# Softmax sums in four strips of 32 columns, and a new place for their reciprocal and the norm

## What is computed

```python
q = jnp.einsum('bnd,hde->bhne', query, Wq) * scale
k = jnp.einsum('bmd,hde->bhme', query, Wk)
v = jnp.einsum('bmd,hde->bhme', query, Wv)
logits = jnp.einsum('bhne,bhme->bhnm', q, k)
attn = jax.nn.softmax(logits, axis=-1)
out = jnp.einsum('bhnm,bhme->bnhe', attn, v)
```

## Time and profile before

| | |
|---|---|
| median of 3 runs | 1893.6 us (1893.3 to 1894.4) |
| the profiled execution | 1892.8 us, its span 1891.0 us |
| TensorE busy (matmul) | 97% |
| GpSimd busy | 71% |
| VectorE busy | 64% |
| ScalarE busy | 45% |

### The profile page before, as it was taken

One profiled execution on the slowest core, in us unless ns is written; L12 is line 12 of the kernel. 1 busy time (PEld: TensorE's weight loads), 2 busy tenths in 40 slices (PEclk: granted clock), 3 DMA queues, 4 the chain that ended last, 5 costly groups with the idle time before them and its releaser, 6 DMA issues.

```text
span 1891.0 us, 30738 instructions
## 1 busy us (share of the span) xinstructions
PE 1837.1 (97%) x11400; PEld 1172.4 (62%) x11400; DVE 1212.2 (64%) x2147; ACT 858.9 (45%) x1101; POOL 1346.7 (71%) x719
## 2 busy tenths in 40 slices
PE   7899999999999999999999999999999999999998
PEld 5555555556666565556666565556665555598887
DVE  5566665566766656856666657766666668665565
ACT  3344444444445444443345544444444534465674
POOL 1688787878667867788578767887668677662564
PEclk9899999999999999999999999999999999999999
DMA  4210000002312000022311000021111011533340
GB/s 139 84 41 20 23 18 23 18 23 68 107 29 60 26 18 24 21 63 85 86 44 42 18 13 23 29 81 55 46 44 38 16 34 35 173 110 132 129 134 34
DMA packets 132142, 104.24 MB, mean 55 GB/s; under 512 B 58140, under 2 KB 118684, under 8 KB 130972
## 3 DMA queue, kind: packets, MB, share of 16 engines
q1 hardware_dynamic: 128924, 93.81, 16.7%
q0 software_dynamic: 3072, 8.46, 1.2%
HBM read 69.15 MB, written 29.43 MB: 52 GB/s over the span
## 4 chain that ended last, share of the span: by engine, by line
PE 84%; POOL 5%; DVE 4%; issue 3%; ACT 2%; DMA 1%; SPq 0%; POOLq 0%; DVEq 0%; ACTq 0%
PE score_ps L1134 23%; PE av_ps L1148 22%; PE spare_ps L1097 9%; PE spare_ps L1113 8%; PE spare_ps L1090 5%; PE spare_ps L441 4%; POOL prob_sum L1018 3%; PE y_ps L1713 3%; PE spare_ps L1159 3%; PE h_ps L1684 3%; DVE max_of L1290 1%; PE spare_ps L490 1%; PE spare_ps L465 1%; POOL w_lo L1446 0%; POOL expert_rows L430 0%
## 5 line engine op out<-in xcount | busy, mean ns | idle before, releaser
L1018 POOL TENSOR_TENSOR prob_sum<-prob_sum,probs 128x1024 f32<-128x1024 f32 (+1 forms) x384 | 907.9, 2364 | 193.6 <-ACT probs L1234 161.3
L1290 DVE TENSOR_REDUCE max_of<-spare_ps 128x1 f32<-128x512 f32 x1024 | 656.5, 682 | 346.0 <-PE spare_ps L1113 335.2
L1234 ACT ACTIVATE probs<-score_ps 128x1024 f32<-128x1024 f32 x512 | 502.7, 1025 | 677.1 <-PE score_ps L1134 669.0
L1148 PE MATMUL av_ps<-probs,v 128*64 128x512 f32 x2048 | 487.9, 602 | 2.1 <-ACT probs L1234 1.4
L1148 PEld LDWEIGHTS av_ps<-probs,v 128*64 128x64 f32 x2048 | 129.8, 136 | 240.5 <-issue 218.4
L1014 POOL TENSOR_TENSOR prob_sum<-probs 128x1024 f32<-128x1024 f32 (+1 forms) x64 | 150.4, 2351 | 137.6 <-ACT probs L1234 137.5
L1113 PE MATMUL spare_ps<-k_hi,q_hi 64*128 64x512 f32 x1024 | 229.2, 441 | 14.7 <-DVE max_of L1290 14.0
L1113 PEld LDWEIGHTS spare_ps<-k_hi,q_hi 64*128 64x128 f32 x1024 | 99.1, 185 | 216.1 <-issue 180.4
L1134 PE MATMUL score_ps<-q_hi,k_hi 64*128 64x512 f32 x1024 | 210.9, 406 | 1.1 <-DVE o_in L1340 0.9
L1134 PE MATMUL score_ps<-shift_rows,ones 64*128 64x512 f32 x1024 | 205.3, 394 | 0.0
L1134 PE MATMUL score_ps<-q_lo,k_hi 64*128 64x512 f32 x1024 | 204.7, 393 | 0.0
(11 more groups left out here) (249 smaller groups left out, 2357.7 us busy)
## 6 DMA issues: line engine op xcount, KB each, us to landing
o_transposed<-o_out SPq DMA_DIRECT2D x64, 256.0 KB, 2.0
v<-in_L_ffn_W_dram SPq DMA_DIRECT2D x16, 1024.0 KB, 5.7
o_in<-o_transposed SPq DMA_DIRECT2D x28, 512.0 KB, 4.1
w_raw<-in_L_attn_Wq_dram SPq DMA_DIRECT2D x64, 64.0 KB, 2.3
w_raw<-in_L_attn_Wk_dram SPq DMA_DIRECT2D x64, 64.0 KB, 2.2
wv_raw<-in_L_attn_Wv_dram SPq DMA_DIRECT2D x32, 128.0 KB, 3.2
shift_rows<-neg_rows SPq DMA_DIRECT2D x256, 1.0 KB
x<-in_x_dram SPq DMA_DIRECT2D x4, 1024.0 KB, 5.9
```

Source lines behind the costliest of these rows:

```text
L1018: pool.tensor_tensor(out, out, probs[:, n % RING, heads], ALU.add).then_inc(prob_added, 1)
L1148: last = pe.matmul(av_ps[hd * E:(hd + 1) * E, :], v[:, quad % 2, kt, 2 * first_head + hd, :], probs[:, n % RING, hd, :], start=(kt == 0), ...
L1234: act.activation(probs[:, n % RING], score_ps[n % 2][:, :, :], ACT.Exp).then_inc(probs_ready, 1)
L1290: dve.tensor_reduce(max_of[:, u % 2, kh, j, hd:hd + 1], bank[:, :], AX.X, ALU.max).then_inc(pass_read, 1)
```

## The change

A sum becomes four matmuls instead of two: each head's 512 queries are cut in two `halves` of 256, and each of the four (head, half) gets a strip of 32 of the bank's partitions, with ones of 32 columns. So the result lies in 256 columns instead of 512, and the transpose out of the bank is half as long. The inverse, however, is wanted on all 64 partitions of a head for all 512 queries: eight copies, written as reductions over an axis of one element, bring each strip's 8 columns to both strips of its head (each 32 partitions x 8 elements). A new semaphore counts them, then one reciprocal of 128x16 follows in place, and the spreading as before. In three lines of `STEPS` the words `recip` and `norm` move.

```diff
 STEPS = tuple(tuple(line.split()) for line in (
-    "early av av av pass score score pass sum av recip pass score score pass late bite bite",
-    "bite norm score pass early av pass score score pass score pass late av av av",
-    "av pass score score pass early av sum pass score score pass bite late av recip av",
+    "early av av av pass score score pass sum av pass score score pass recip late bite norm bite",
+    "bite score pass early av pass score score pass score pass late av av av",
+    "av pass score score pass early av sum pass score score pass recip bite late av av",
     "pass norm score score pass early bite bite av pass score score pass late av av av"))
...
+    HALF = BANK // 2
+    HEAD_HALVES = ((0, 0), (0, 1), (1, 0), (1, 1))
...
+    def strip(hd, half):
+
+        return slice((2 * hd + half) * BLOCK, (2 * hd + half + 1) * BLOCK)
...
-                for hd in range(2):
-                    last = pe.matmul(bank[hd * E:(hd + 1) * E, :], ones[:, 0:E], prob_sum[:, u % 2, hd, :],
-                                     start=True, stop=True)
+                for hd, half in HEAD_HALVES:
+                    last = pe.matmul(bank[strip(hd, half), 0:HALF], ones[:, 0:BLOCK],
+                                     prob_sum[:, u % 2, hd, half * HALF:(half + 1) * HALF], start=True, stop=True)
                 last.then_inc(sum_ready, 1)
...
-                dve.transpose(sums[:, :], bank[:, :]).then_inc(sum_turned, 1)
+                dve.transpose(sums[:, 0:HALF], bank[:, 0:HALF]).then_inc(sum_turned, 1)
 
             def invert(u):
                 dve.wait_ge(sum_turned, u + 1)
-                dve.reciprocal(inverse[:, :], sums[:, 0:BANK:BLOCK]).then_inc(recip_done, 1)
+                blocks = HALF // BLOCK
+                for hd, half in HEAD_HALVES:
+                    for other in range(2):
+                        dve.tensor_reduce(inverse[strip(hd, other), half * blocks:(half + 1) * blocks],
+                                          sums[strip(hd, half), 0:HALF:BLOCK].rearrange("p (c a) -> p c a", a=1),
+                                          AX.X, ALU.add).then_inc(sum_copied, 1)
+                dve.wait_ge(sum_copied, 2 * len(HEAD_HALVES) * (u + 1))
+                dve.reciprocal(inverse[:, :], inverse[:, :]).then_inc(recip_done, 1)
                 dve.wait_ge(recip_done, u + 1)
                 dve.transpose(sums[:, :].rearrange("p (c t) -> p c t", t=BLOCK),
```

More of the change, by code:

```diff
@@ L861, in build_attention @@
         sum_turned = sem("sum_turned")
+        sum_copied = sem("sum_copied")
         recip_done = sem("recip_done")
```

## The result

The changed kernel takes 1925.1 us (median of 4 runs, 1924.0 to 1929.9), the kernel before beside it 1894.0 (1893.3 to 1895.1). The ratio is 1.0166, with a 95% interval of 1.0153 to 1.0178. So it is 1.7% slower, where 0.4% faster was forecast, and it lies outside the range. The profiled execution has a span of 1924.4 us against 1891.0: 33.4 more.

What follows compares the result with a forecast made beforehand. TensorE was taken as the bound, busy 1837.1 of 1891.0 us, with VectorE's order mattering inside a half. −19.2 + 11.4 + 0.2 = −7.6 us gave 1885.2 profiled, 1886.0 median, 0.4% faster; range 1874 to 1908.

Steps and rivals of the forecast that it cites:

- The order of TensorE does not change: In the changed `STEPS`, TensorE, ScalarE and GpSimd keep their steps and only VectorE's order moves; no time of its own.
- Term 1, the sum: Sums on TensorE: four strips abreast save 0.427 us, a change of width costs 0.13; 0.30 each, 19.2 us for 64.
- no price for the change of width: Rival at TensorE's sums: changing column width is free, or k1's bank is no bound; 8 to 11 us less, 1876, chance 0.14.
- two at a time: Rival at TensorE's sums: only two strips run abreast, so a sum still streams 0.855 us; 1913 us, chance 0.12.
- abreast with a loss: Rival at TensorE's sums: four strips need 0.55 us rather than 0.43, 8 us in all; 1894, no change, chance 0.09.
- Term 2, the copies: VectorE's work behind a sum: transpose 0.27 us shorter, eight copies 0.09 us apart added; chain through the spreading 1.75 us.
- Term 3, the first line: VectorE's chain behind the first line's last pass delays low parts that free banks: 0.28 us per light half, 11.4 in all.
- VectorE's queue becomes the bound of the pass: Rival in the first line: copies 0.21 us apart, chain 0.85 longer, 24 halves lose 0.85 each; 1906 us, chance 0.15.
- its point of 0.14 us: Distance between VectorE's copies from which the slower rival decides, at 0.32 us more chain.
- the 20 that I had named as the bound: Sign: TensorE's waits for k_lo are some 10 us in all; the forecast is wrong if they exceed 20 us.
- Term 4, the third line: Chain covered by bite, late steps and value products: nothing; if cover fails, up to 1 us in nine split halves.
- The tail: Last sum, norm and store ahead of the tail's loads: +0.55 in copies and transpose, −0.3 in the sum, +0.2 us.

Runs made afterwards that it cites:

- experiment 1: The kernel before with only the three changed lines of `STEPS`, without strips and copies: 1893.0 us, ratio 0.9996.
- Experiment 3: The changed kernel with two copies over all 128 partitions instead of eight, leaving out the exchange between strips: 1876.0 us, ratio 0.9909.
- experiment 5: The changed kernel with the reciprocal first, then only the four copies that cross between strips, same result: 1886.2 us, ratio 0.9954.
- experiment 4: The changed kernel with eight copies that each stay in their own strip, leaving out the exchange: 1896.6 us, ratio 1.0016.
- experiment 6: As experiment 5, but with reciprocal and crossing copies ahead of the last maxima and the spreading as its own step behind them: 1881.6 us, ratio 0.993.
- experiment 7: The changed kernel with the eight copies as `tensor_copy` instead of reductions over one element: 2271.9 us, ratio 1.1992.
- experiment 8: The changed kernel with the old third line of `STEPS` put back: 1936.8 us, ratio 1.0218.

## Why the prediction was wrong

- *The order of TensorE does not change*: right, as experiment 1 shows.
- *Term 1, the sum*: right. Forecast 0.30 us a sum, 19.2 in all. Measured 0.29 in the first line and 0.26 in the third, 17.6 in all, and 17 between experiments 1 and 3. In the third line the change of width costs 0.10 us into the sum (start of the last value product to the sum, 0.52 for 0.42) and the rest out of it, so "no price for the change of width" is out, as are "two at a time" and "abreast with a loss".
- *Term 2, the copies*: this step failed first. "I take 0.09, since the copies are unconnected" took its rows from instructions over all 128 partitions, which all start in the same group of 32. The copies do not, and none overlaps: 0.19 us, near the other end of the bounds. Chain 2.40 us, not 1.75. The transpose out of the bank was right, 446 ns for 711. With a chain of about the forecast length (experiment 5) the forecast time came true within 0.2 us, and part of that is luck: its chain was 0.13 us shorter, lines 1 and 2 took 6.5 us more than before where the terms give about 2, lines 3 and 4 13.2 less where they give about 9, and the tail 2.4 more where they give 0.2.
- *Term 3, the first line*: the mechanism was right, and it is the rival *VectorE's queue becomes the bound of the pass* that came about, past its point of 0.14 us. Its size was wrong: with 0.21 us a copy it gave 1906, and 0.19 made 1925. Its 2.4 us for each 0.1 us of chain holds only at the start (2.2). It counted 24 halves and the wait alone; its 3 × 1.5 is 4.5 and not 4.6, which moves nothing. Missing were, in a light half, a slower start behind the wait (pass to product 0.43 for 0.32 us); 1.9 us of wait at place 16 and the fallen clock behind it, so that these halves lost 3.05, 3.30 and 1.90 us (no fall behind the third) with the sum's gain already taken off, instead of 1.5 each before it; waits of bite v at places 20 and 24 of 0.5 and 1.0 us instead of 0.13 and 0.6; and the half h = 124, which I set aside because it "has no bites": its value product waits for the norm, and it lost 3.7 us. Experiment 1 puts 1.0 of these to the new place of the norm. The waits for k_lo came to 17.0 us for about 10, inside the 20 that I had named as the bound; that sign was too weak, since it left out q_lo, the maxima and the clock.
- *Term 4, the third line*: "nothing" failed too. I looked only at the passes, and there is a bite v behind the first one whose bank waits for its maxima. In the regular halves it takes back 0.08 us of the sum's 0.26; three of the nine with a split lost 6.5 us, where I had priced up to 1 each as a mishap. The 0.9 us back, three times, that I named as the best case came in experiment 1, without the copies. No third line shows a wait for k_lo, as forecast; it waits for maxima and q_lo.
- *The tail*: forecast +0.2 us, measured +4.6. Its length varies from 254.3 to 263.2 us over kernels with nearly the same work there. A fall of the clock 135 to 138 us behind the last sum stood in it here (1799.3 us) and in experiments 4, 6, 7 and 8, with tails of 257.8 to 263.2 us; without that fall the tails are 254.3 to 259.8. So the fall goes with a longer tail, but does not set its length alone. What sets the tail stays open.

In sum: −17.6 for the sums, and about +36 in lines 1 and 2 (27.2 + 9.0 of gain) and +10 in lines 3 and 4 (2.0 + 7.8), and +4.6 in the tail. Experiment 3 shows how much of this goes with the length of the copies: with two of them lines 1 and 2 take 735.4 us, 27.7 less, and lines 3 and 4 762.3, 15.9 less. About 8.5 us in lines 1 and 2 stay beside the sums' gain of 9.0; 3.8 of them are the new places (experiment 1), the rest was not taken apart.

## What to carry to other kernels

Before small instructions on VectorE are costed as overlapping, look at the partitions where each starts; a row of ones over all partitions says nothing of ones that move data between groups of 32. Arrange such an exchange with as few instructions as possible, and put it where the engine would idle (here ahead of the last maxima), not in front of what frees a buffer. And cost a growing stall with more than its own length: behind five of seven waits of 1.9 us and more the work ran at half clock here for 3.4 us, and steps that I had taken as covered came out from under their cover. Look also at the last round of a loop, where the steps that covered a wait elsewhere are missing (h = 124).

## What the runs showed of the hardware

- VectorE: eight 32x8 instructions that change the group of 32 partitions of their output, or of input and output, start 0.19 us apart (changed kernel), in the same group 0.08 (experiment 4).
- VectorE beside GpSimd: a copy of 32x8 took 0.70 us on average and 2.92 at the most (experiment 7); those over 0.4 us ended, but for 4 of 211, 0.02 to 0.04 us after a GpSimd instruction. As a sum over one element it took 0.15 on average and 0.17 at the most.
- VectorE beside GpSimd: the split of 128x1024 (L513) took 3.35 us at 875.97, ending 1.09 us after GpSimd's addition; with GpSimd idle it took 1.21 to 1.23.
- TensorE: four strips of 32 columns with 256 columns each run abreast, 0.24 us from the first four to the second four and 0.57 us from the first of eight to the next product.
- TensorE: behind five of seven waits of 1.9 to 4.0 us the granted clock was 0.50 (1.2 GHz) for 3.4 us.
